# Turning twelve tiles on TensorE, a SyncE queue of transposes only, and a router per four tiles, in a fused layer of LayerNorm, attention and mixture of experts

## The chip, the cores and the metric

One Trainium2 chip, all 8 cores, every core with its own 4096 rows of the input and no traffic between cores. The time is the device time of the slowest core in microseconds (us). Lower is better. Weights and inputs are float32 in HBM; the matmuls run in bfloat16 with float32 sums.

## What is computed

The reference, cut to what matters (C = 1024, 16 heads of 64, 8 experts of width 128, shared expert of width 256, 6 of 8 experts taken):

```python
xn = (x - mean(x)) / sqrt(var(x) + 1e-5)
# attention on every 4th row of a segment of 2048 rows (512 rows), causal
q, k, v = split(xn[:, :, ::4] @ w_in.T + b_in)
a = softmax(causal(q @ k.T / 8)) @ v @ w_out.T + b_out      # other rows: 0
# feed-forward on every row
shared = (silu(xn @ ws1) * (xn @ ws2)) @ ws3
topk_w, topk_i = top_k(softmax(xn @ wr), 6);  topk_w /= sum(topk_w)
h = silu(xn @ w1[e]) * (xn @ w2[e])                         # all 8 experts
routed = sum_e w_full[:, e] * (h[e] @ w3[e])
out = x + a + shared + routed
```

## The kernel before

**Tiles.** The 4096 rows of a core are two segments of 2048; a tile is 128 rows, 32 tiles in all. `GROUPS` (line 30) puts four tiles of one residue together; tiles 12 to 15 and 28 to 31 are the rows on which attention runs, for segment 0 and 1.

**One order for all engines.** `steps()` (line 66) yields the steps of the whole program, and each engine's program is a loop over it that does its own part of each step. So every engine and every DMA queue works in the order of `steps()`, and a wait in one step holds back all that stands later on that engine.

**The steps.** `ln_stat` reads a tile of x (DVE statistics; ACT takes the square root with one table load, and the next silu needs another). `ln_norm` writes the normalised tile in bfloat16 to `xn_tm` (two buffers), and SP turns it by a DMA transpose into `XN` (line 321). `gu` is one unit of the first feed-forward matmuls: `s0` and `s1` are halves of the shared expert (264 and 256 columns, s0 with the 8 router columns), 0 to 3 are pairs of experts (512 columns). Each is 8 matmuls on PE (line 452) into one of six PSUM banks, a silu on ACT (line 690), a product on DVE (lines 602 and 629) into a piece buffer `hst`, and a DMA transpose by SP into `HT` (line 336): five transposes for each tile. The router (lines 585 to 620) runs on DVE once for each tile, in thirteen small operations. `down` multiplies `HT` by `W3` (line 472, 20 matmuls of 512 columns), and for attended tiles also `OFM` by `Wo` (line 476); DVE adds it to `res` (line 643). SP then stores `res` to out (line 356) and loads x into the `res` slot of tile m + 2 (line 311). `res` has three slots.

**Attention.** For each of 8 pairs of heads: `qk` (line 493), four `score` steps (lines 522, 525) with a maximum on DVE (line 660) and exp on ACT (line 724) into one of three `Pb` buffers, `pnorm` (DVE divides, line 670; SP turns the block by a DMA transpose into `PT`, line 349) and `av` of the pair before (line 543). One `down` step stands in each pair of heads, between `pnorm 2` and `pnorm 3`. So SP gets, in this order: transpose 2, the store and the load of `down`, transpose 3.

**Weights.** POOL starts all weight loads (they cast to bfloat16). `Wsh`, `Wgu` 0 to 3 and `W3` are started at the beginning, one behind the other. `Wqk` and `Wv` follow when tile 15 is normalised, `Wo` when the units of tiles 4 to 11 are through. A partition's row of a weight tensor is one contiguous run in HBM: 16 KB for `Wgu` and `Wv`, 8 KB for `Wqk`, 40 KB for `W3`. Loads of x are in runs of 4 KB.

**The order around the change.** LayerNorm of tiles 0 to 3; `s0`, `s1` of tiles 0 to 3 (with LayerNorm of 4 to 7); units 0 of tiles 0 to 7, units 1, then 2 and 3 for tiles 0 to 11, with the LayerNorm of later tiles in between; `down` 0 to 3; attention of segment 0 with `down` 4 to 11; tiles 12 to 27; attention of segment 1 with `down` 20 to 27; tiles 28 to 31 and their `down`.

## Times and profile before

| | us |
|---|---|
| median of 3 runs | 822.77 (821.97 to 835.91) |
| profiled execution, its own time | 831.12 |
| its span on the slowest core (core 3) | 829.6 |
| spans of the other cores | 801.2 to 819.5 |
| PE busy in that span | 614.3 (74%) |
| DVE busy | 377.4 (45%) |
| ACT busy | 248.7 (30%) |

The profile is of one execution, on its slowest core. PE is the matmul queue of TensorE, DVE is VectorE, ACT is ScalarE, POOL is GpSimd and SP is SyncE; SPq is SP's queue issuing DMAs. Times in rows count from the start of the span. The granted clock (PEclk) is 1.00 at 2.4 GHz and 0.5 at 1.2 GHz, averaged over a stretch. "Idle before, releaser" says what ended the idle time of an engine. The chain of waits is followed back from the last instruction to whatever released it.

### The profile page before, as it was taken

How to read it: one execution, taken by the hardware profiler on the slowest of the kernel's cores; microseconds unless marked ns; L12 is line 12 of the kernel's file. 1: busy time of each engine (PE TensorE's matmuls, PEld its weight loads, DVE VectorE, ACT ScalarE, POOL GpSimd, SP SyncE). 2: the span in 40 equal slices, each digit the busy share in tenths (PEclk: the TensorE clock that was granted, in tenths of full speed). 3: DMA queues.
4: the chain of work that ended last, by engine and by line, in shares of the span. 5: the costliest groups of instructions: out<-in, count | busy, mean ns of one | idle time of the engine just before them, and what ended most of it. 6: DMA issues, size and time to landing. Idle time of an engine off the chain costs nothing.

```text
span 829.6 us, 12117 instructions; the slowest of 8 cores (801.2 to 829.6 us)
## 1 busy us (share of the span) xinstructions
PE 614.3 (74%) x3136; PEld 294.6 (36%) x3136; DVE 377.4 (45%) x1232; ACT 248.7 (30%) x620; POOL 36.3 (4%) x48
## 2 busy tenths in 40 slices
PE   0006497898049689665699999998839878758998
PEld 0004153443014234322345445554414334323543
DVE  2006575754021444335354556766643545534531
ACT  0003425344001434233333224334423434332200
POOL 3000000001000000000101100000000000011002
PEclk9998899999569899879799999999979999877999
DMA  8996526349998977997326545664424975553123
GB/s 181 185 173 166 112 52 138 70 111 150 117 102 212 153 124 138 139 135 179 82 60 163 144 112 146 172 153 104 109 56 84 172 153 120 123 116 81 38 71 101
DMA packets 140866, 103.60 MB, mean 125 GB/s; under 512 B 124912, under 2 KB 124928, under 8 KB 139392
## 3 DMA queue, kind: packets, MB, share of 16 engines
q1 hardware_dynamic: 136704, 79.73, 44.6%
q0 software_dynamic: 4096, 23.10, 18.3%
q8 instruction: 28, 0.46, 0.3%
q14 instruction: 38, 0.31, 0.2%
HBM read 79.21 MB, written 16.78 MB: 116 GB/s over the span
## 4 chain that ended last, share of the span: by engine, by line
PE 43%; DMA 22%; DVE 11%; SPq 10%; issue 8%; ACT 5%; DVEq 1%; ACTq 0%
PE PS L452 17%; PE PS L472 14%; DMA PT<-Pb 14%; SPq L336 7%; DMA XF<-x 7%; PE PS L476 3%; ACT L690 3%; DVE bns L558 3%; PE PS L493 2%; PE PS L504 2%; DVE hst L629 2%; PE PS L543 2%; DVE res L643 1%; SPq L321 1%; PE PS L522 1%
## 5 line engine op out<-in xcount | busy, mean ns | idle before, releaser
L452 PE MATMUL PS<-Wgu,XN 128*128 128x512 bf16 x768 | 178.6, 392 | 12.1 <-DVE hst L602 7.5
L472 PE MATMUL PS<-W,HT 128*128 128x512 bf16 x560 | 135.9, 398 | 0.0
L629 DVE SCALAR_TENSOR_TENSOR hst<-sil,gate,PS 128x128 bf16<-128x128 bf16 x256 | 72.6, 343 | 100.5 <-ACT sil L690 56.7
L452 PEld LDWEIGHTS PS<-Wgu,XN 128*128 128x128 bf16 x768 | 76.5, 100 | 106.3 <-issue 26.1
L724 ACT ACTIVATE Pb<-PS,nmx 128x128 bf16<-128x128 f32 (+3 forms) x128 | 66.1, 524 | 134.9 <-DMA PT<-Pb 69.4
L452 PE MATMUL PS<-Wsh,XN 128*128 128x264 bf16 (+1 forms) x384 | 48.0, 281 | 67.6 <-DMA XN<-xn_tm 63.5
L660 DVE TENSOR_REDUCE nmx<-PS 128x2 f32<-128x256 f32 (+1 forms) x64 | 51.1, 819 | 80.1 <-PE PS L525 80.1
L690 ACT ACTIVATE sil<-PS 128x256 bf16<-128x256 f32 (+1 forms) x192 | 60.6, 349 | 80.3 <-PE PS L452 68.9
L472 PEld LDWEIGHTS PS<-W,HT 128*128 128x128 bf16 x560 | 57.0, 103 | 69.0 <-issue 11.9
L643 DVE TENSOR_TENSOR res<-PS,res 128x512 f32<-128x512 f32 x64 | 43.7, 690 | 82.4 <-PE PS L472 40.3
L493 PE MATMUL PS<-XN,Wqk 128*128 128x512 bf16 x256 | 65.3, 414 | 12.3 <-DMA XN<-xn_tm 12.3
L452 PE MATMUL PS<-Wgu,Wo 128*128 128x512 bf16 x256 | 60.6, 395 | 12.7 <-DVE hst L629 9.5
L681 ACT ACT_TABLE_LOAD x28 | 35.9, 1283 | 100.8 <-DVE rs L566 90.0
L452 PEld LDWEIGHTS PS<-Wsh,XN 128*128 128x128 bf16 x384 | 38.1, 100 | 78.9 <-issue 69.7
L543 PE MATMUL PS<-PT,Vs 128*64 128x256 bf16 x192 | 17.0, 332 | 49.2 <-DMA PT<-Pb 49.2
L690 ACT ACT_TABLE_LOAD x30 | 38.5, 1283 | 26.0 <-PE PS L452 25.6
L472 PE MATMUL PS<-W,PT 128*128 128x512 bf16 x80 | 19.7, 410 | 33.0 <-DMA PT<-hst 32.5
L493 PEld LDWEIGHTS PS<-XN,Wqk 128*128 128x128 bf16 x256 | 26.5, 106 | 45.0 <-issue 22.6
L452 PEld LDWEIGHTS PS<-Wgu,Wo 128*128 128x128 bf16 x256 | 25.5, 101 | 44.6 <-issue 18.0
L670 DVE TENSOR_SCALAR Pb<-Pb,rz 128x128 bf16<-128x128 bf16 (+3 forms) x128 | 33.9, 308 | 6.9
L706 ACT ACTIVATE Ks<-PS,bqk_sb 128x512 bf16<-128x512 f32 x16 | 11.0, 687 | 84.0 <-PE PS L493 83.9
L522 PE MATMUL PS<-Ks,Qs 64*128 64x128 bf16 (+3 forms) x128 | 22.1, 341 | 18.8 <-ACT Pb L724 18.8
(60 smaller groups left out, 466.8 us busy)
## 6 DMA issues: line engine op xcount, KB each, us to landing
res<-x SPq DMA_DIRECT2D x32, 512.0 KB, 5.8
out<-res SPq DMA_DIRECT2D x32, 512.0 KB, 3.6
XF<-x SPq DMA_DIRECT2D x24, 512.0 KB, 4.8
Wqk<-wqk POOLq DMA_DIRECT2D x16, 512.0 KB, 6.9
Wqk<-x SPq DMA_DIRECT2D x8, 512.0 KB, 5.3
Wgu<-wgu POOLq DMA_DIRECT2D x4, 1024.0 KB, 30.7
Wv<-wv POOLq DMA_DIRECT2D x4, 1024.0 KB, 14.6
W<-w POOLq DMA_DIRECT2D x1, 2560.0 KB, 54.4
```

Of the source, the lines that this page charges most:

```text
L336: sy.dma_start_transpose(out=ht_at(n)[:, b:b + 2, :], in_=hst[:, i % NPIECE, :]).then_inc(d_h[i % NPIECE], 16)
L452: ins = t_.matmul(PS[:, b, 0:nk], xn[:, ci, :], w[:, ci, k0:k0 + nk], start=(ci == 0), stop=(ci == CI - 1))
L472: ins = t_.matmul(PS[:, h, :], ht[:, k, :], W3[:, k, cols], start=(k == 0), stop=(k == NB - 1 and not 0 <= attended < 4))
L493: ins = t_.matmul(PS[:, b, :], Wqk[:, n % NWQK, ci, 128 * k:128 * (k + 1)], XN[:, s0:s0 + 4, ci, :], start=(ci == 0), stop=(ci == CI - 1))
L543: ins = t_.matmul(PS[64 * h:64 * (h + 1), b, 256 * half + q0:256 * (half + 1)], Vs[:, c, 128 * hp + 64 * h:128 * hp + 64 * (h + 1)], PT[:, ...
L629: ins = v.scalar_tensor_tensor(h[:, 128 * k:128 * (k + 1)], s[:, 128 * k:128 * (k + 1)], gate[:, n % 16, e:e + 1], PS[:, b, 256 + 128 * k: ...
L643: v.tensor_tensor(res[:, sl, cols], PS[:, h, :], res[:, sl, cols], op=ALU.add).then_inc(v_add, 1)
L660: v.tensor_reduce(nmx[:, i % 4, :], PS[:, b:b + 2, 0:128 * (j + 1)], axis=AX, op=ALU.max, negate=True).then_inc(v_mx, 1)
L670: ins = v.tensor_scalar(out=pp, in0=pp, scalar1=rz[:, i % 4, h:h + 1], scalar2=None, op0=ALU.mult)
L681: s.activation(out=sd[:, n % 4:n % 4 + 1], in_=mv[:, n % 4, 1:2], func=AF.Sqrt, bias=EPS).then_inc(a_sd, 1)
L690: s.activation(out=sil[:, i % 4, 0:nk], in_=PS[:, b, 0:nk], func=AF.Silu).then_inc(a_sil, 1)
L724: s.activation(out=Pb[:, i % NPB, 0:j + 1, h, :], in_=PS[:, b + h, 0:128 * (j + 1)].rearrange("p (c k) -> p c k", c=j + 1), func=AF.Exp, b ...
```

## The change

- **Turning.** The normalised tiles 0 to 15 are turned on PE (8 transposes of 128x128 for each tile, into bank 0 or 1) and evicted by ACT (new steps `xt`). For tiles 0 to 11 the pieces `s1`, 0 and 1 are turned on PE too (2 transposes each, step `ht`, evicted by ACT); pieces 2 and 3 of these tiles stay DMA transposes. For tiles 12 to 31 the four pieces of the experts go in one DMA transpose of 128x1024 and the shared piece in another: two for each tile in place of five.
- **Queues.** SP issues transposes only, but for the first four loads of x. All other loads of x, the loads of `res` and the stores of out are issued by POOL.
- **Router.** `s0` of four tiles, then one ranking for all four, then `s1` of four tiles with the gate behind the first: 12 operations of DVE and one tanh for four tiles, and four copies of the router columns.
- **LayerNorm.** From tile 4 on two tiles share one square root on ACT. Tiles 16 to 19 are normalised inside the attention of segment 0.
- **Attention.** `pnorm 3` stands ahead of `down`.
- **Weights.** Every weight is laid out in HBM so that a run is 4 KB. The loads are spread over the steps, `Wqk` has two buffers for three, `Wo` is loaded after the attention of segment 0.

```diff
+BATCH = [(0,), (1,), (2,), (3,)] + [(n, n + 1) for n in range(4, NTILE, 2)]
+def shared_steps(g):
+    for n in range(4 * g, 4 * g + 4):
+        yield ("gu", n, "s0")
+    yield ("rank", g)
+    for n in range(4 * g, 4 * g + 4):
+        yield ("gu", n, "s1")
+        if n == 4 * g:
+            yield ("gate", g)
...
         yield ("pnorm", seg, hp, 2)
+        yield ("pnorm", seg, hp, 3)
         yield ("down", fill + hp)
-        yield ("pnorm", seg, hp, 3)
+        if seg == 0 and hp in (1, 4):
+            yield ("ln_stat", BATCH_OF[16 + 2 * (hp == 4)])
+        if seg == 0 and hp in (2, 5):
+            yield ("ln_norm", BATCH_OF[16 + 2 * (hp == 5)])
...
+    yield ("w", "u1")
+    yield from shared_steps(0)
+    yield ("ht", 0, "s1")
     for n in range(4):
         yield ("gu", n, 0)
+        if n < 3:
+            yield ("ht", n + 1, "s1")
+        if n % 2 == 0:
+            yield ("ln_stat", BATCH_OF[4 + n])
+            yield ("ln_norm", BATCH_OF[4 + n])
+        else:
+            yield ("xt", 3 + n)
+            yield ("xt", 4 + n)
+        if n > 0:
+            yield ("ht", n - 1, 0)
...
+    for g in range(3, 7):
+        yield from shared_steps(g)
+        if g == 3:
+            yield ("av", 0, 7)
+        for n in range(4 * g, 4 * g + 4):
+            for u in range(4):
+                yield ("gu", n, u)
+                if g > 3 and n % 2 == 0 and u == 0:
+                    yield ("ln_stat", BATCH_OF[n + 4])
+                if g > 3 and n % 2 == 0 and u == 2:
+                    yield ("ln_norm", BATCH_OF[n + 4])
+            if g in (4, 5):
+                yield ("down", n - 4)
...
+def by_pe(n, u):
+    return n < 12 and u in ("s1", 0, 1)
...
 # SP
-                    elif st == "down":
-                        (m,) = at
-                        sy.wait_ge(v_add, 2 * m + 2)
-                        sy.dma_start(out=o_of(m), in_=res[:, m % NRES, :]).then_inc(d_out[m % NRES], 16)
-                        if m + 2 < NTILE:
-                            load_res(m + 2)
+                        elif u == 3:
+                            k = H_AT[(n, 0)][1]
+                            sy.wait_ge(v_h, GU_NO[(n, u)] + 1)
+                            sy.dma_start_transpose(
+                                out=ht_at(n)[:, 0:8, :],
+                                in_=hse[:, k:k + 4, :].rearrange("p a b -> p (a b)")).then_inc(d_h[("e", k)], 16)
...
 # POOL
-                    gp.dma_start(out=Wqk[:, n % NWQK], in_=dwqk[n % 8]).then_inc(d_wqk[n % NWQK], 16)
+                    gp.dma_start(out=Wqk[:, n % NWQK].rearrange("p (a b) k -> p a b k", a=2),
+                                 in_=dwqk[n % 8].rearrange("a p b k -> p a b k")).then_inc(d_wqk[n % NWQK], 16)
...
+                    if st == "ln_norm":
+                        for n in BATCH[at[0]]:
+                            k = n + 4 if n < 14 else n + 2
+                            if n in (14, 15) or k >= NTILE:
+                                continue
+                            gp.wait_ge(v_xn, n + 1)
+                            load_x(k)
...
                     elif st == "down":
+                        gp.wait_ge(v_add, 2 * m + 2)
+                        gp.dma_start(out=o_of(m), in_=res[:, m % NRES, :]).then_inc(d_out[m % NRES], 16)
+                        if m + 2 < NTILE:
+                            load_res(m + 2)
...
 # PE
+                    elif st == "xt":
+                        t_.wait_ge(v_xn, n + 1)
+                        bank_wait(b)
+                        for ci in range(CI):
+                            ins = t_.transpose(ps_bf16(b)[:, ci, :], xn_tm[:, n % 2, P * ci:P * (ci + 1)], ident[:])
+                        ins.then_inc(p_tr, 1)
+                    elif st == "ht":
+                        t_.wait_ge(v_h, GU_NO[(n, u)] + 1)
+                        bank_wait(b)
+                        for k in range(2):
+                            ins = t_.transpose(ps_bf16(b)[:, k, :], h_at(n, u)[:, P * k:P * (k + 1)], ident[:])
+                        ins.then_inc(p_tr, 1)
...
 # ACT
+                    elif st == "xt":
+                        s.wait_ge(p_tr, i + 1)
+                        s.activation(out=xn_at(n), in_=ps_bf16(i % 2), func=AF.Identity).then_inc(a_tr, 1)
```

In the stretch from unit 1 of tiles 0 to 7 on, the pairs of `ln_stat` and `ln_norm` stand behind the units of tiles 1 and 3 (unit 1) and 2 and 6 (unit 2), and their two `xt` steps one unit later (unit 1) or two units later (unit 2).

## Rows read from the trace of the kernel before

**Rows 1.** Busy time by stage; columns: stretch, each engine's busy us, clock, DMA share, GB/s
```profile
0.00:62.10 62.10, 0.00 (x0) 0.03 (x1) 7.91 (x18) 2.10 (x5) 6.38 (x19) 1.00 0.98 179
62.10:259.00 196.90, 136.66 (x656) 67.46 (x657) 93.66 (x349) 59.02 (x122) 2.65 (x5) 0.85 0.65 121
259.00:413.70 154.70, 114.03 (x602) 51.18 (x601) 65.16 (x170) 52.88 (x157) 9.96 (x12) 0.87 0.83 139
413.70:621.90 208.20, 187.15 (x969) 94.42 (x968) 121.47 (x444) 73.18 (x154) 4.69 (x2) 0.97 0.50 122
621.90:761.00 139.10, 111.75 (x601) 50.60 (x602) 65.93 (x168) 53.04 (x157) 7.89 (x8) 0.88 0.63 126
761.00:829.60 68.60, 64.67 (x312) 30.91 (x311) 23.24 (x85) 8.54 (x25) 4.70 (x2) 0.97 0.24 65
```

**Rows 2.** Timeline of the start; columns: start us, us, engine, line, instruction
```profile
18.00 1.28 DVE L558 BATCH_NORM_STATS2 bns<-Wqk 128x6 f32<-128x512 f32 x2 [7.00 <-DMA Wqk<-x]
...
21.76 36.88 SPq L321 DMA_TRANSPOSE XN<-xn_tm  x1
25.83 1.29 DVE L558 BATCH_NORM_STATS2 bns<-Wqk 128x6 f32<-128x512 f32 x2 [5.26 <-DMA Wqk<-x]
...
62.10 7.30 PE L452 MATMUL PS<-Wsh,XN 128*128 128x264 bf16 x48 [62.10 <-DMA XN<-xn_tm]
```

**Rows 3.** Timeline ahead of the first down step
```profile
239.09 15.21 PE L472 MATMUL PS<-W,PT 128*128 128x512 bf16 x60 [32.55 <-DMA PT<-hst]
```

**Rows 4.** Chain of waits in attention of segment 0; columns: start us, us, what
```profile
381.56 0.74 PE PS L543 x12
382.30 0.32 PE PS L522 x2
382.62 0.22 PE PS L525 x2
382.84 4.33 PE PS L472 x20
...
389.01 5.11 DMA PT<-Pb
```

**Rows 5.** Chain of waits: matmuls in a row at either level of the clock
```profile
259.19 3.45 PE PS L493 x16
...
287.85 5.14 PE PS L493 x16
```

**Rows 6.** Chain of waits in tiles 12 to 19
```profile
486.66 8.68 PE PS L452 x48
495.34 4.32 PE PS L472 x20
```

**Rows 7.** Timeline of DVE in tiles 24 to 27
```profile
559.68 1.28 DVE L558 BATCH_NORM_STATS2 bns<-XF 128x6 f32<-128x512 f32 x2
...
561.50 0.81 DVE L570 TENSOR_SCALAR xn_tm<-XF,mv,rs 128x1024 bf16<-128x1024 f32 x1 [0.18 <-DVE rs L566]
...
570.47 1.28 DVE L558 BATCH_NORM_STATS2 bns<-XF 128x6 f32<-128x512 f32 x2
```

**Rows 8.** Timeline of one unit behind PE, in units 3 of tiles 0 to 11
```profile
199.78 0.38 ACT L690 ACTIVATE sil<-PS 128x256 bf16<-128x256 f32 x1 [1.34 <-PE PS L452]
200.41 0.61 DVE L629 SCALAR_TENSOR_TENSOR hst<-sil,gate,PS 128x128 bf16<-128x128 bf16 x2 [1.12 <-ACT sil L690]
```

**Rows 9.** DMA issues of the page; columns: count, KB written each, median us to landing
```profile
res<-x SPq DMA_DIRECT2D x32, 512.0 KB, 5.8
out<-res SPq DMA_DIRECT2D x32, 512.0 KB, 3.6
...
Wgu<-wgu POOLq DMA_DIRECT2D x4, 1024.0 KB, 30.7
...
W<-w POOLq DMA_DIRECT2D x1, 2560.0 KB, 54.4
```

**Rows 10.** Busy time of core 5 in the dense stretch; columns as in Rows 1
```profile
454.00:540.00 86.00, 86.00 (x455) 44.35 (x454) 52.41 (x188) 31.85 (x67) 0.00 (x0) 1.00 0.60 157
```

More of the change, by code:

```diff
@@ L89, in steps @@
+    yield ("ht", 7, 1)
+    yield ("w", "u3")
+    yield ("w", "w3")
+    yield from shared_steps(2)
+    yield ("ht", 8, "s1")
+    for u in (0, 1):
+        for n in range(8, 12):
+            yield ("gu", n, u)
+            if u == 0 and n < 11:
+                yield ("ht", n + 1, "s1")
+            if n > 8:
+                yield ("ht", n - 1, u)
+            elif u == 1:
+                yield ("ht", 11, 0)
     for n in range(12):
         yield ("gu", n, 2)
-        if n % 3 == 2:
-            yield from ln_step(12 + n // 3)
+        if n == 0:
+            yield ("ht", 11, 1)
+        if n in (2, 6):
+            yield ("ln_stat", BATCH_OF[12 + (n == 6) * 2])
+            yield ("ln_norm", BATCH_OF[12 + (n == 6) * 2])
+        if n in (4, 8):
+            yield ("xt", 12 + (n == 8) * 2)
+            yield ("xt", 13 + (n == 8) * 2)
@@ L284, in build_nc @@
         a_av = sem("a_av")
+        a_tr = sem("a_tr")
         def wait_x(eng, n):
[L287 to L299 removed]
+            if n < 4:
+                eng.wait_ge(d_x0[n], 16)
+            elif n < 16:
+                eng.wait_ge(d_x[n % 4], 16 * (n // 4))
+            else:
+                eng.wait_ge(d_x[n % 2], 16 * (3 + (n - 16) // 2 + 1))
         with nc.Block() as block:
@@ L622, in _ @@
[L622 to L626 removed]
+                        else:
+                            v.wait_ge(v_zg, 7 * (n // 4) + 7)
                             for k in range(2):
```

463 lines of the change are left out of this document (267 added, 196 removed).

## The prediction, made before the changed kernel was run

> **What bounds the kernel now.** I read the busy time by stage first, since one share for the whole span says nothing of where PE waits [rows 1]. PE is idle for 62 us, then busy 136.7 of 196.9 us at a granted clock of 0.85. It is nearly full only in tiles 12 to 27 and at the end. Both attention stages leave 27 to 41 us idle, at a clock below 0.9. So the question in each stage is what PE waits for.
>
> The timeline of the start shows it [rows 2]. Tiles 0 and 1 are normalised early, but SP sits for 36.88 us on one transpose, and the first matmul begins at 62.10. Meanwhile POOL's queue moves Wsh, four Wgu and W3; W3 lands 54.4 us after its issue [rows 9]. Tiles 2 and 3 of x are there only at 18.00 and 25.83. The same happens ahead of the first `down`: PE waits 32.55 us for a transpose of a piece [rows 3], just when Wqk, Wv and Wo are being loaded.
>
> In attention the chain of waits goes in a ring: `down` on PE 4.33, the addition on DVE, then SP's store and load, then the transpose 5.11, then `av`, a score, `down` again [rows 4]. The transpose of score 3 is held by `down`, which it doesn't need. In tiles 12 to 19 the chain is PE alone: 8.68 us for a tile's six units and 4.32 for `down` [rows 6]. In tiles 24 to 27 a tile takes 10.79 us (570.47 less 559.68), since router and LayerNorm stand on DVE between two tiles [rows 7].
>
> **The floor of PE at full clock.** A tile's units 8.68; `down` 4.32 for 20 matmuls, for an attended tile 16 more, so 7.78 [rows 6]; `qk` 3.45 and a `v` half of it, 1.73 [rows 5]; a 128-column matmul 0.11, 0.22 for two [rows 4].
> Tiles 0 to 11: 12 x 8.68 = 104, `down` 4 x 4.32 = 17. Added: `xt` of tiles 4 to 15, 12 x 8 x 0.11 = 11, and 36 `ht` steps of two, 36 x 2 x 0.11 = 8. Together 140.
> One attention stage: 8 x 3.45 + 8 x 1.73 + 8 x 4.32 = 76, scores and `av` some 19 (32 scores with masks, on average 0.4 from the longest at 0.54; 8 `av` at 0.74) [rows 4]: 95.
> Tiles 12 to 27: 16 x 8.68 + 4 x 7.78 + 4 x 4.32 = 187. End: 65 busy [rows 1].
> Sum 140 + 95 + 187 + 95 + 65 = 582.
>
> **The start: 62 becomes 20.** x in runs of 4 KB lies beside weights in runs of 16 KB. Tiles 2 and 3 (1.05 MB) came in from about 8 to 25.8 us, 59 GB/s, while all loads to 62 us (weights 15.8 MB, bias and six tiles 3.6 MB) went at about 312 GB/s [rows 2, 9]. That is a fifth of the whole, as if the queues took turns run by run. With runs of 4 KB on both sides x gets half: 1.05 MB at 156 GB/s is 7 us, tile 3 is there at 15.5; Wsh (2.1 MB) at about 16. Statistics, root, normalising (1.3 + 0.2, 0.5, 0.8) and the turn of tile 3 with its eviction take 4.5: first unit at 20. All four `xt` stand before the first unit, so the last tile counts. If the runs change nothing, tile 3 comes at 25.8 and the first unit at 30.6; if only the last tile of x counts, 18. I take 20.
>
> **Stage to the first `qk`: 197 becomes 180.** PE needs 140. Against it stands a new wait. An `xt` needs the tile normalised, and PE works in order. A unit's product is done about 1.45 us after PE has left it (silu 0.38, products 0.61, gaps) [rows 8]. Then DVE does two tiles' statistics (2 x 1.28 + 0.4), waits for the root behind a table load (1.6), and normalises (0.2 + 0.81) [rows 7]: 5.7, so 7.2 us after the unit. PE has one unit and one or two `ht` (1.95 to 2.2) until the first `xt` in four cases, two units (3.5) in two. Waits 4 x 5.2 + 2 x 3.7 = 28. Each also costs clock: after a wait 16 matmuls took 5.14 against 3.45 [rows 5], 1.7; for six about 9. Eviction of a whole turned tile isn't in the trace: between one silu of 256 columns, 0.38, and four of them, 1.5 [rows 8]; 16 of these are 6 to 24 us on ACT, which is busy 59 of 197 [rows 1] and loses table loads. I take 1.1, off the path; uncovered, it adds 1.1 at the start and nothing behind. The 24 transposes left to SP for pieces 2 and 3 run beside W3. Eight piece buffers give them eight units (13.8 us) of slack; beyond that a late transpose holds DVE. The 32.55 goes: `down` 0 to 3 need pieces sent 20 us or more earlier. `down` 2 and 3 still wait some 3 us for `res`, whose load follows the store. 140 + 28 + 9 + 3 = 180. Bounds: 143 with the waits filled, 195 if DVE is two units behind each time.
>
> **Attention of segment 0: 155 becomes 115.** `pnorm 3` no longer waits for `down` on DVE nor on SP. The ring is then `av` 0.8, score 0.5, maximum and exp about 3.0, division 0.9, transpose 5.1 to 5.9: 10.8 per pair of heads, against 95 / 8 = 11.9 of PE. PE bounds, narrowly. I add 1.3 for each pair (10), 4 for two LayerNorm batches with two changes of table each (4 x 1.28, half of it beside other work), 4 for Wv and Wqk at the beginning and 2 for the clock. Bounds: 103 and the 155 of before.
>
> **Tiles 12 to 27: 208 becomes 190.** 187, and 3 for the change from attention. The router falls from 13 operations a tile to 16 for four tiles and the root to one table pair for two, so 10.79 goes to 8.68. Its latency lies under four `s1` units and the six banks. Behind the rank DVE still has 52 of 86 us [rows 10]. **Attention of segment 1: 139 becomes 111**, as before but with no LayerNorm. **End: 69 stays**; PE is the chain there, and the last store through POOL may cost half a microsecond.
>
> **Sum.** 20 + 180 + 115 + 190 + 111 + 69 = 685 of span, against 829.6. The profiled execution took 831.12, the median of the runs is 822.77: 1% lower. So 685 x 822.77 / 829.6 = 679.
>
> **Edits at nothing.** Stores and loads through POOL: POOL is busy 36 of 830 us and what it then waits for (an addition, a product of `qk`) comes in the same order as on PE. What stands behind a waiting `down` on POOL is the next Wqk load and the next x; two buffers of Wqk and two to four of x leave them a pair of heads, 12 us. If that cover were gone, each late Wqk load costs its whole landing.
>
> **Rivals.** (a) *Attention stays at its pace.* The ring was never held by order but by the DMA engines: their share is 0.83 and 0.63 there [rows 1], and the same bytes in less time raise it. For it: it would be 0.83 x 155 / 115, above 1, in segment 0. Against: that share held Wo (4 MB), now elsewhere, and time in which runs wait for each other; in the dense stretch 0.60 was enough for 153 GB/s [rows 10]. It gives 155 + 139 in place of 115 + 111: 679 + 67 = 746.
> (b) *The clock gives way* when all cores are full at once. At the 0.85 seen in [rows 1] the 582 us of PE become 685: 782. Against it: in the dense stretch core 5 ran 86.00 of 86.00 us at 1.00 [rows 10], all others like it.
> The Trainium skill, "TensorE: Matmul & The Clock Gate", Part 1, says that three or more cores of a die with dense matmuls take the die to thirteen sixteenths of the clock. By that rule the sum would be 134 us more, 813, not faster by 2%. The trace does not agree: 1.00 over 86 us.
> (c) *Slower: the `res` ring through POOL.* A slot of `res` is stored, then loaded, in one queue with all weights; three tiles take one store and one load. Now 3.6 + 5.8 [rows 9], no bound. If each of POOL's transfers takes L, a tile takes 2L/3. The first `down` comes at about 180; the kernel is slower once 32 tiles need more than 650 us, 20.3 each, L = 30.6. That is the landing of a Wgu at the start, 30.7 [rows 9]: then 180 + 32 x 20.5 = 836 of span, 829. Against it: such times belong to a queue filled with 15 MB.
> The Trainium skill, "SBUF — State Buffer", section "SBUF: two separate sides", says that descriptors of POOL's transfers are held up while DVE works in a mode with both ports. It gives no price for this mix; it speaks for (c), and no row here shows such a hold.
> (d) *The runs of 4 KB don't help*, and transposes beside weights stay slow: start 30.6, 10 more in both stages before tile 12: 710.
>
> **Chances.** Forecast 0.62, own range 645 to 712, from its bounds: waits in stage two filled (-30) or longer (+15), attention +-8 each. (d) 0.11. (a) 0.16, (b) 0.06, (c) 0.03, and 0.02 for a small change through something not seen. Two per cent is about what a measurement of this kernel can tell from no change. (a), (d) and, but for 0.01 of it with a still lower clock, (b) are faster by more: 0.62 + 0.11 + 0.16 + 0.05 = 0.94. Within 2% 0.03 (that 0.01 and the unseen 0.02), slower 0.03. Range 642 to 746: up to (a), leaving out (b), (c) and half of (a).
>
> **What would show it.** First unit near 20 us (start right); waits of PE for DVE's normalising, six of 3.5 to 5.5 us; no long wait ahead of `down` 0; `down` steps 12 to 13.5 us apart in attention, with the chain on PE; tile periods of 8.7 in tiles 24 to 27. Wrong if PE waits for `PT` in most pairs of heads (a), if the granted clock is under 0.95 where PE is full (b), if DVE waits for `res` or for x from POOL (c), or if x lands after 25 us (d).

## The result, and the profile after

The changed kernel is faster, by much less than forecast. Its median is 763.45 us of 4 runs (760.16 to 766.15) against 827.33 us of 4 runs of the kernel before beside them (821.97 to 835.91): a ratio of 0.925, 95% interval 0.916 to 0.934. The prediction was 679 us, range 642 to 746. The direction was right; the size was not.

Busy time by stage of the changed kernel on its slowest core (core 7, span 758.6), cut at the same marks as [rows 1]; columns as there:
```profile
0.00:21.10 21.10, 3.75 (x32) 3.07 (x33) 9.47 (x20) 4.78 (x8) 6.79 (x19) 1.00 0.89 176
21.10:205.00 183.90, 148.90 (x828) 80.52 (x827) 74.79 (x229) 66.06 (x144) 15.16 (x26) 0.90 0.62 121
205.00:366.60 161.60, 117.11 (x642) 54.23 (x640) 75.05 (x195) 59.34 (x168) 22.75 (x34) 0.83 0.84 151
366.60:569.50 202.90, 184.71 (x928) 91.78 (x928) 88.10 (x270) 47.23 (x110) 20.86 (x29) 0.96 0.69 118
569.50:691.30 121.80, 108.68 (x641) 51.51 (x642) 65.58 (x176) 53.76 (x162) 16.03 (x24) 0.96 0.81 150
691.30:758.60 67.30, 60.50 (x273) 26.90 (x272) 15.23 (x40) 6.83 (x17) 10.24 (x9) 0.96 0.23 66
```

The marks behind each attention need care: up to `av` of the last pair the kernel before had one unit to do, the changed one has eight (some 7 us of PE), so these rows carry them in the attention. At marks that mean the same in both (the first unit behind the last `qk`), on the same two cores:

| stage | before, core 3 | after, core 7 | change | predicted change | miss |
|---|---|---|---|---|---|
| start | 62.1 | 21.2 | -41 | -42 | +1 |
| to the first `qk` | 196.9 | 183.7 | -13 | -17 | +4 |
| attention of segment 0 | 143.7 | 151.7 | +8 | -40 | **+48** |
| tiles 12 to 27 | 219.3 | 212.9 | -6 | -18 | +12 |
| attention of segment 1 | 130.4 | 111.8 | -19 | -28 | +9 |
| end | 77.3 | 77.3 | 0 | 0 | 0 |
| span | 829.6 | 758.6 | -71 | -145 | +74 |

The start gave what was promised, and the stage behind it nearly. Core 3 was the longest of the kernel before in the second and the third stage, so this pair of cores flatters both: by the medians over all cores (next section) the changes are -43, -9, +16, -6, -20 and +1. Attention of segment 0 gave nothing: it is the stage in which LayerNorm, all four kinds of loads and the transposes of P lie together, at a DMA share of 0.84 and the lowest clock, 0.83. Its chain of waits (columns as in [rows 4]), where the transposes of P stand:
```profile
219.44 8.00 DMA PT<-Pb
...
268.59 10.17 DMA PT<-Pb
...
294.36 23.30 DMA PT<-Pb
317.67 0.35 issue
318.01 1.28 PE PS L704 x12
...
332.55 10.23 DMA PT<-Pb
```
The transpose of [rows 4] took 5.11 us; here the chain meets 8 to 23 us, and DMA of P is 32.0% of this stage's chain, 52 us. The waits of the same stretch say the same from the side of ACT and PE (columns: engine, line, waited for: us in total, times, longest us):
```profile
ACT Pb L906 <- DMA PT<-Pb: 37.0, 6, 7.8
...
PE PS L683 <- ACT Pb L906: 24.7, 6, 6.8
...
PE PS L704 <- DMA PT<-Pb: 15.3, 1, 15.3
```
The typical transpose of P is hardly slower than before: over all cores the median in this stage, from issue to landing, was 5.5 us and is 5.7. The late ones became more: 39 of 249 took over 10 us against 14 of 248, and 21 took over 12 us against 6.

In some executions one die showed a lower granted clock than the other and took longer: the ratios below leave these out, the medians do not, and where the profiled one was such (b1, e10, g2, f1, a0) its stages were read on the other die too, and the text gives attention 0 there where it differs by over 2 us.

### The profile page after: what moved, and what is told of

Same layout as the page of the kernel before. It is cut to its first block, busy times and chain, and to the rows that moved or that the text cites. A ratio compares the mean times of both kernels' runs of the same rounds, so it can differ in the third digit from the quotient of the medians.

```text
span 758.6 us, 11591 instructions; the slowest of 8 cores (735.3 to 758.6 us)
## 1 busy us (share of the span) xinstructions
PE 623.7 (82%) x3336; PEld 308.0 (41%) x3336; DVE 328.2 (43%) x930; ACT 238.0 (31%) x608; POOL 91.8 (12%) x140
## 4 chain that ended last, share of the span: by engine, by line
PE 50%; DMA 20%; DVE 12%; issue 8%; ACT 6%; SPq 2%; DVEq 1%; ACTq 0%; POOLq 0%; POOL 0%
PE PS L589 25%; DMA PT<-Pb 11%; PE PS L633 10%; PE PS L656 4%; PE PS L637 4%; DMA HT<-hse 3%; PE PS L667 3%; ACT Pb L906 3%; DVE bns L720 3%; DMA XN<-xn_tm 3%; DMA Wqk<-x 2%; PE PS L602 2%; SPq L426 2%; DVE xn_tm L737 1%; PE PS L704 1%
## 5 line engine op out<-in xcount | busy, mean ns | idle before, releaser
L589 PE MATMUL PS<-Wgu,XN 128*128 128x512 bf16 x768 | 174.3, 386 | 4.4 <-DVE hse L798 4.4
L798 DVE SCALAR_TENSOR_TENSOR hse<-sil,gate,PS 128x128 bf16<-128x128 bf16 x256 | 76.1, 343 | 159.8 <-ACT sil L860 141.8
L633 PE MATMUL PS<-W,HT 128*128 128x512 bf16 x560 | 131.1, 388 | 1.5 <-DVE res L812 1.5
L860 ACT ACTIVATE sil<-PS 128x256 bf16<-128x256 f32 (+1 forms) x192 | 64.0, 349 | 203.8 <-PE PS L589 177.6
L633 PEld LDWEIGHTS PS<-W,HT 128*128 128x128 bf16 x560 | 55.4, 100 | 67.3 <-issue 7.5
L589 PE MATMUL PS<-Wsh,XN 128*128 128x256 bf16 (+1 forms) x384 | 47.0, 286 | 8.7 <-DMA XN<-xn_tm 8.7
L555 POOL DMA_DIRECT2D out<-res x32 | 17.9, 561 | 287.2 <-DVE res L812 286.8
L602 PE MATMUL PS<-ident,xn_tm 128*128 128x128 bf16 x128 | 15.2, 308 | 45.3 <-DVE xn_tm L737 45.3
L683 PE MATMUL PS<-Ks,Qs 64*128 64x128 bf16 (+3 forms) x128 | 21.2, 326 | 34.6 <-ACT Pb L906 34.5
L835 DVE RECIPROCAL rz<-zz 128x2 f32<-128x2 f32 x64 | 10.4, 162 | 76.4 <-ACT Pb L906 76.4
L507 POOL DMA_DIRECT2D XF<-x x22 | 11.7, 532 | 207.6 <-DVE xn_tm L737 206.5
```

The source lines that it names most:

```text
L589: ins = t_.matmul(PS[:, b, 0:nk], xn[:, ci, :], w[:, ci, k0:k0 + nk], start=(ci == 0), stop=(ci == CI - 1))
L602: ins = t_.transpose(ps_bf16(b)[:, ci, :], xn_tm[:, n % 2, P * ci:P * (ci + 1)], ident[:])
L633: ins = t_.matmul(PS[:, h, :], ht[:, k, :], W3[:, k, cols], start=(k == 0), stop=(k == NB - 1 and not 0 <= attended < 4))
L798: ins = v.scalar_tensor_tensor(h[:, 128 * k:128 * (k + 1)], s[:, 128 * k:128 * (k + 1)], gate[:, n % 16, e:e + 1], PS[:, b, 256 + 128 * k: ...
L860: s.activation(out=sil[:, i % 4, 0:nk], in_=PS[:, b, 0:nk], func=AF.Silu).then_inc(a_sil, 1)
```

## How the runs are compared

All stage times below are medians over the eight cores of one profiled execution, in us, at marks that can be found alike in every kernel: the first unit, the first `qk`, the first unit behind the last `qk`, the first `qk` of segment 1, the first unit behind its last `qk`, the end. The cores of one run lie within 4 us of each other at the start, but within 4 to 24 us in attention 0 (widest in e7, 140.8 to 164.3). So I read differences of 7 and more between medians, and take smaller ones as a hint only; attention 0 of b1 (111.6 to 133.4) and of b2 (135.9 to 153.1) do not overlap. Kernels of one batch ran on one chip, and each ratio is to the runs of before in its own batch, whose median was 835.6 to 841.4; so medians of different batches are not compared, ratios are. The 161 and 122 us in the expectations of e1 to e4 are the attention stages of core 7 up to `av` of the last pair, as in the rows above; in the table they are 148.6 and 112.0.

| kernel | start | to `qk` | att. 0 | 12-27 | att. 1 | end | median | ratio to before |
|---|---|---|---|---|---|---|---|---|
| before | 63.4 | 187.6 | 132.3 | 218.5 | 131.7 | 76.6 | 827.33 | 1 |
| after | 20.4 | 179.0 | 148.6 | 213.0 | 112.0 | 77.2 | 763.45 | 0.925 |
| a0 after again | 20.8 | 182.7 | 149.7 | 211.8 | 113.0 | 77.4 | 768.03 | 0.912 (.902-.923) |
| b1 before + new order | 63.6 | 189.0 | 124.8 | 212.9 | 112.9 | 71.8 | 792.97 | 0.944 (.931-.958) |
| b2 = b1 + POOL's queue | 65.6 | 183.5 | 142.9 | 214.7 | 115.9 | 79.8 | 817.70 | 0.980 (.969-.990) |
| b3 before + short runs | 30.2 | 204.3 | 133.6 | 217.7 | 131.4 | 77.5 | 801.29 | 0.962 (.952-.972) |
| e2 after, long runs | 31.1 | 183.3 | 159.2 | 213.2 | 115.8 | 81.8 | 797.28 | not given |
| e10 after, old order | 20.5 | 188.5 | 153.8 | 213.4 | 140.9 | 75.6 | 813.89 | not given |
| e1 after, x/res/out on SP | 21.0 | 184.8 | 137.9 | 208.5 | 111.3 | 75.9 | 753.57 | 0.900 (.887-.912) |
| e3 after, LayerNorm out | 20.4 | 181.1 | 129.7 | 223.3 | 118.6 | 77.5 | 760.84 | 0.906 (.889-.923) |
| e9 after, no table change | 20.5 | 187.3 | 146.0 | 210.8 | 111.8 | 77.3 | 776.17 | 0.927 (.914-.941) |
| e4 after, no `Wqk` reloads | 20.6 | 179.3 | 130.1 | 211.8 | 107.2 | 80.0 | 748.01 | 0.889 (.875-.903) |
| e6 after, bare attention | 20.7 | 180.1 | 103.9 | 224.2 | 104.9 | 80.1 | 725.04 | 0.861 (.851-.871) |
| e7 after, four `Pb` | 20.7 | 180.5 | 147.5 | 210.4 | 109.4 | 77.3 | 772.86 | 0.913 (.901-.925) |
| e5 after, five transposes | 20.7 | 178.9 | 152.1 | 200.5 | 117.7 | 77.3 | 757.24 | 0.903 (.897-.910) |
| f1 = e1 + e5 | 21.0 | 185.1 | 140.8 | 207.2 | 107.8 | 76.1 | 753.84 | 0.900 (.887-.912) |
| f2 = f1, loads deferred | 21.0 | 184.0 | 134.5 | 207.3 | 110.4 | 76.8 | 746.90 | 0.889 (.878-.901) |
| g1 = f2, LayerNorm moved | 21.3 | 202.4 | 110.0 | 207.4 | 109.7 | 76.6 | 744.93 | 0.890 (.875-.905) |
| g2 = g1, moved further | 21.1 | 196.4 | 111.9 | 207.8 | 110.8 | 76.0 | 737.43 | not given |
| g3 = g2, `res` 2 early | 20.9 | 194.0 | 108.6 | 207.8 | 110.4 | 76.2 | 731.68 | 0.883 (.873-.894) |

a0 shows how well a kernel repeats itself: up to 4 us in a stage, and 0.912 against 0.925 in the ratio.

## Experiments on the steps that held

**b1: the new order alone**, in the kernel before.
```diff
         yield ("pnorm", seg, hp, 2)
-        yield ("down", fill + hp)
         yield ("pnorm", seg, hp, 3)
+        yield ("down", fill + hp)
```


> The kernel before with one part of the change alone: pnorm 3 ahead of down in each pair of heads. The prediction took the ring (down, addition, SP's store and load, transpose 3, av) as what bounds attention, with 5.7 us of it removable by this order. Theory O (order): both attention stages shorter by 25 us or more together, ratio 0.97 or less. Theory B (the transposes come late because other transfers run beside them): under 10 us together, ratio 0.985 to 1.0.

Attention 0 went from 132.3 to 124.8, attention 1 from 131.7 to 112.9, the ratio to 0.944. One moved line is worth more than half of the whole change's gain. So the order did hold the attention of segment 1. In attention 0 its 7.5 us are no more than the cores differ among themselves, and 124.8 is still some 20 above the forecast, whose 115 is 104 at these marks (11 us less, as 154.7 and 143.7 on core 3). That stage had something else in it even with the old queues and no LayerNorm inside.

**e10: the changed kernel with the old order.** The same two lines put back.

> The changed kernel with the down-projection ahead of the fourth normalising, as before. b1 showed the swap to give 7.5 us in attention 0 and 18.8 us in attention 1 in the kernel before. If it is worth as much here, attention 0 is 156 to 160 and attention 1 126 to 134, 25 to 35 us in all, ratio .955 to .965. If in attention 0 the late transfers bound the pace whatever the order (theory: TensorE waits for the turned P there, not for its bank), attention 0 stays at 149 to 153 and only attention 1 grows by 12 to 19; ratio .94 to .95.

Attention 1 grew by 28.9, attention 0 by 5.2 (2.1 on cores 4 to 7), and the best run was 799.89. Core 5, whose mean granted clock of 0.915 is among those of the changed kernel's cores (0.914 to 0.935), has 141.4 in attention 1, so the growth is not the clock's. In the changed kernel the order is worth even more in attention 1, and nothing that can be told from noise in attention 0: there something else was the bound.

**b3: short runs alone**, in the kernel before: all weight arrays in runs of 4 KB, e.g.
```diff
-                    gp.dma_start(out=Wgu[:, u], in_=dwgu[u]).then_inc(d_wgu[u], 16)
+                    gp.dma_start(out=Wgu[:, u].rearrange("p (a b) k -> p a b k", a=4),
+                                 in_=dwgu[u].rearrange("a p b k -> p a b k")).then_inc(d_wgu[u], 16)
```


> The kernel before with the weight arrays laid out in 4 KB runs and nothing else. If runs of 4 KB give the activations beside them a larger share (forecast, and e2's +11 us at the start when undone), the fourth tile of x lands 5 to 10 us earlier, the time to the first unit falls from 63 to 50 to 57, and attention 0 is 5 to 10 us shorter than 132; ratio .965 to .985. If the share doesn't hang on the run length, the ratio is 1.00 +- .01.

The first unit came at 30.2 in place of 63.4, far more than I expected. The timeline of SP's queue shows why (columns as in [rows 2]); the transpose whose issue took 36.88 us there takes 11.08:
```profile
16.15 11.08 SPq L321 DMA_TRANSPOSE XN<-xn_tm  x1
27.28 2.84 SPq L323 DMA_DIRECT2D XF<-x  x1
30.83 17.09 SPq L321 DMA_TRANSPOSE XN<-xn_tm  x1
```
But the next ones still take 17.09, and the stage to the first `qk` gives 17 of the 33 back. Attention did not move (133.6), against my 5 to 10.

**e2: the changed kernel with the old long runs.** b3's edit the other way round.

> The changed kernel with the weights laid out in HBM as before (runs of 8 to 40 KB in place of 4 KB). If short runs are what lets transposes and loads of x through: first unit at 28 to 31 us in place of 21, attention of segment 0 longer by 10 or more, kernel 780 to 800. If short runs cost DMA time (more packets for the same bytes) and that is the loss in attention: attention of segment 0 shorter by 10 or more, kernel under 755.

Start 31.1 against 20.4, attention 0 +10.6 (+4.6 on cores 4 to 7), in all 27 us of span. The statistics of the fourth tile of x begin at 26.33 with long runs and at 16.43 with short ones (first row e2's, second row the changed kernel's timeline):
```profile
26.33 1.29 DVE L716 BATCH_NORM_STATS2 bns<-Wqk 128x6 f32<-128x512 f32 x2 [4.26 <-DMA Wqk<-x]
```
```profile
16.43 1.29 DVE L720 BATCH_NORM_STATS2 bns<-Wqk 128x6 f32<-128x512 f32 x2 [0.55 <-DMA Wqk<-x]
```
With b3 this is a small square: the kernel before 63, short runs alone 30, all of the change but short runs 31 (turning on TensorE, and the weight loads spread over the steps, which no run parts), all of it 20. Either side removes most of the long wait; together they add only 10 more.

## Experiments on the step that failed

Three suspects for attention 0: the transfers of x, `res` and out now in POOL's queue; the weight reloads beside them; LayerNorm of tiles 16 to 19 inside.

**e6: attention without the last two.** No reloads of `Wqk` and `Wv` (all heads use the weights that were loaded first), LayerNorm with its loads of x moved behind the attention. The loads of `res` and the stores of out stay in POOL's queue.
```diff
-                        if n + NWQK < 16:
-                            load_wqk(n + NWQK)
-                        if kc == 3 and i < 3:
-                            load_wv(i + 1)
-        if seg == 0 and hp in (1, 4):
-            yield ("ln_stat", BATCH_OF[16 + 2 * (hp == 4)])
-        if seg == 0 and hp in (2, 5):
-            yield ("ln_norm", BATCH_OF[16 + 2 * (hp == 5)])
```


> The changed kernel with most of what runs beside the transposes of P taken out of attention: only two of 16 loads of Wqk and one of four of Wv are made (later heads use those weights, so this part of the result is not the reference's), and the LayerNorm of tiles 16 to 19 stands in the units of tiles 12 to 15. Singly, no Wqk took 18.5 us off the attention of segment 0 and no LayerNorm 19. Theory B+L (competing transfers and LayerNorm together are the whole loss): 149 falls by 38 or more, to 105 to 112, what the forecast had (115 less the last av). Theory R (the ring of three P buffers with a latency of 5 us for each transpose bounds by itself): it stays at 118 or more, and segment 1 at 105 or more.

Attention 0 fell from 148.6 to 103.9. The run's slowest core in that stretch (columns as in [rows 1]) and its waits for P:
```profile
205.00:309.00 104.00, 97.78 (x559) 44.28 (x567) 59.49 (x148) 49.78 (x151) 10.79 (x17) 0.97 0.62 132
```
```profile
ACT Pb L896 <- DMA PT<-Pb: 9.8, 6, 2.9
```
TensorE is busy for 98 of 104 us, and no transpose of P took over 8 us on any core. So the work of attention itself has the pace I forecast, and the miss is what lies beside it. Eight loads of `res` and eight stores went through POOL's queue here too: by themselves they cost nothing that shows. The next ones part it.

**b2: POOL's queue alone**, on top of b1.
```diff
 # SP
-                        sy.dma_start(out=o_of(m), in_=res[:, m % NRES, :]).then_inc(d_out[m % NRES], 16)
-                        if m + 2 < NTILE:
-                            load_res(m + 2)
 # POOL
+                        gp.wait_ge(v_add, 2 * m + 2)
+                        gp.dma_start(out=o_of(m), in_=res[:, m % NRES, :]).then_inc(d_out[m % NRES], 16)
+                        if m + 2 < NTILE:
+                            load_res(m + 2)
```
The loads of x from tile 4 on move in the same way.

> The kernel before with the fourth normalising ahead of the down-projection (as in b1) and, new, all loads of x from tile 4 on, of the residual and all stores issued by GpSimd; the weight loads keep their long runs. If the move to GpSimd's queue costs by itself (theory), attention of segment 0 is 5 to 15 us longer than b1's 124.8, the transpose of a normalised tile takes 6 us or more instead of 3.1, and the ratio is .955 to .98 against b1's .944. If the move is free, as the forecast had it, attention 0 is 125 +- 3 and the ratio .944 +- .01. The first tiles may start later too, since x of tiles 4 to 7 now stands behind the weights in GpSimd's order; that is read from the first stages and kept apart.

Attention 0 went from 124.8 to 142.9, the ratio from 0.944 to 0.980. No byte more is moved, no wait is added on SP, and in neither run does PE wait for a load of `Wqk` in that stage, on any core. The DMA issues of the two pages, first b1, then b2 (columns: what, queue, count, KB written each, median us to landing):
```profile
res<-x SPq DMA_DIRECT2D x32, 512.0 KB, 5.9
...
Wqk<-wqk POOLq DMA_DIRECT2D x16, 512.0 KB, 7.6
...
HT<-hst SPq DMA_TRANSPOSE x140, 2.4
...
PT<-Pb SPq DMA_TRANSPOSE x64, 4.6
...
XN<-xn_tm SPq DMA_TRANSPOSE x24, 3.1
```
```profile
res<-x POOLq DMA_DIRECT2D x32, 512.0 KB, 6.8
...
Wqk<-wqk POOLq DMA_DIRECT2D x16, 512.0 KB, 10.2
...
HT<-hst SPq DMA_TRANSPOSE x140, 2.4
...
PT<-Pb SPq DMA_TRANSPOSE x64, 5.9
...
XN<-xn_tm SPq DMA_TRANSPOSE x24, 5.9
```
The transpose of a normalised tile lands in 5.9 us in place of 3.1; in attention 0 alone that of P goes from 5.0 to 7.3. The transposes of the pieces (`HT`), on whose signal no plain transfer starts, keep their 2.4 us, though most of them lie outside the attention: not every transpose is slower for sharing the DMA engines with POOL's queue. This is an edit that the prediction put at nothing.

The Trainium skill, "DMA: Bandwidth & Descriptors", section "Issuing engines are not separate DMA queues", says that transfers issued from different engines interleave on the same DMA engines and that using several issuers only saves issue time. These two runs show more: who issues decides what a transfer lies beside (3.1 against 5.9 us, and 18 us in the stage). Its section "Queues, rings and completion order" says that a DMA engine takes turns between the queues that have work, a packet at a time. By that rule a transpose shares its turns with whatever POOL's queue holds at that moment. The rows of `XN` and P agree, but would also agree with plain collisions in time (below).

**e1: the changed kernel with these transfers back on SP.** The reverse of b2's edit, and the loads of x behind SP's transposes.

> The changed kernel with one part undone: the loads of x and res and the stores of out are issued by SP again, in the order of the steps. In the changed kernel the attention of segment 0 takes 161 us where 115 were forecast. Theory Q (two queues take turns on the DMA engines, so a transpose that used to be alone behind plain transfers of its own queue now shares every turn with them): attention of segment 0 falls to 140 or less, the median transpose of P lands in under 5 us, the kernel takes 740 or less. Theory B (the DMA engines are simply full of bytes in that stage): 161 stays within 5, kernel 763 +- 8. Theory S (SP's order was the loss in the kernel before): SP waits for additions again, attention of segment 1 goes from 122 back towards 139, kernel 780 or more.

Attention 0 148.6 to 137.9, tiles 12 to 27 213.0 to 208.5, ratio 0.900; the 740 us that the expectation gave for this theory did not come (753.57). The transpose of a normalised tile (first e1's row, then the changed kernel's):
```profile
XN<-xn_tm SPq DMA_TRANSPOSE x16, 3.3
```
```profile
XN<-xn_tm SPq DMA_TRANSPOSE x16, 8.6
```
On SP a load of x is issued behind the transpose; on POOL it starts on the same signal, `v_xn`, beside it. Whether the queue or the simultaneous start costs the 5 us is not settled: both change together in b2 and in e1.

**e3: LayerNorm out of attention**, to the units of tiles 12 to 15.
```diff
-                if g > 3 and n % 2 == 0 and u == 0:
+                if n % 2 == 0 and u == 0:
                     yield ("ln_stat", BATCH_OF[n + 4])
```


> The changed kernel with the LayerNorm of tiles 16 to 19 (four loads of x, two changes of the ACT table there and back, four transposes) taken out of the attention of segment 0 and put into the units of tiles 12 to 15. Theory L (this work is what holds attention): attention of segment 0 falls from 161 to 135 or less, kernel 745 or less. Theory B (bytes): 3.1 of 24.4 MB go, 161 falls by 10 to 20 and tiles 12 to 27 give part of it back, kernel 750 to 760. If neither: 161 +- 5.

Attention 0 148.6 to 129.7, but tiles 12 to 27 213.0 to 223.3 and attention 1 +6.6. LayerNorm costs the attention 19 us, not the 4 of the sum, and the two stages behind give 17 of them back (760.84, ratio 0.906; the time of theory B and not of theory L). It does not act by making P land later. In attention 0 alone, on the slowest core, first e3, then the changed kernel:
```profile
PT<-Pb SPq DMA_TRANSPOSE x31, 5.4
```
```profile
PT<-Pb SPq DMA_TRANSPOSE x31, 5.5
```
and ACT's waits for P there, as the median over the cores, are 41 us in e3 and 37 in the changed kernel.

**e9: the same LayerNorm without its change of table.** The root of tiles 16 to 19 is replaced by a copy on ACT, so that no table is loaded.
```diff
+                        fn = AF.Identity if BATCH[k][0] in (16, 18) else AF.Sqrt
```


> The changed kernel in which the root of tiles 16 to 19 is replaced by a plain copy, so that ACT changes no table in the attention of segment 0; these four tiles are then scaled wrongly, and nothing else changes (same loads, same transposes, same DVE work). Taking the whole LayerNorm out had shortened that stage by 19 us. Theory T (the two changes of table in the row of exps): at least 8 of the 19 come back here. Theory B (its 3 MB of loads and transposes): under 4.

146.0 against 148.6 (148.2 and 142.2 on the two dies): the table is little or nothing of the 19. What remains is DVE's own work in order ahead of the division of P, four more transposes ahead of P's in SP's queue, and four loads of x; which of the three weighs most wasn't tried singly. In the changed kernel's chain of waits both of the first two stand right ahead of a late transpose of P:
```profile
263.46 0.82 DVE xn_tm L737
264.41 1.62 SPq L426
...
266.18 2.26 SPq L426
...
268.59 10.17 DMA PT<-Pb
```

**e4: no reloads of `Wqk`.**
```diff
-                        if n + NWQK < 16:
-                            load_wqk(n + NWQK)
```


> The changed kernel in which only the first two of the 16 loads of Wqk are made; the later pairs of heads use the weights of the first two, so 14 MB of reads are left out and all engines' work stays. Theory B (bytes): attention of segment 0 falls from 161 by 25 to 45, of segment 1 from 122 to about 105, kernel about 700 to 720. Theory L (LayerNorm's changes of table and DVE time in attention): 161 falls by less than 10. Theory Q: falls by 10 to 20, since one of two competing streams is halved.

All later pairs of heads use the first two `Wqk`. 130.1: 18.5 us less, with LayerNorm and POOL's queue as they were. Here P does land sooner: ACT's waits for it halve, from 37 to 19 us (medians over the cores), and 17 transposes in place of 72 take over 8 us. Attention 1 gains 4.8. LayerNorm and these reloads are 37.5 of the 44.7 us that e6 takes out; the two reloads of `Wv` and the interplay hold the other 7. The 11 us of e1 do not belong to that sum, since e6 leaves `res` and out in POOL's queue: what that queue costs hangs on what else is there.

**e7: four `Pb` buffers.** `NPB = 3` becomes 4, in case ACT only lacked a place to write.

> The changed kernel with four P buffers in place of three, nothing else. Theory R (ACT waits for the buffer of three scores before, so every late transpose stops the scores): attention of segment 0 falls by 10 or more, of segment 1 by 4 or more, kernel 745 to 753. Theory B (the DMA engines can't deliver sooner): both within 4, since PE then waits for the same transposes in av.

147.5: nothing. Though ACT is recorded as waiting for the transpose to free `Pb`, a fourth buffer doesn't help, since `av` needs the same transposes a moment later: ACT's waits for P fell from 37 to 28 us and PE's rose from 13 to 20 (medians over the cores). The wait row named the right transfer and the wrong remedy.

**e5: the four pieces of tiles 12 to 31 turned one by one again.**
```diff
-                            sy.dma_start_transpose(
-                                out=ht_at(n)[:, 0:8, :],
-                                in_=hse[:, k:k + 4, :].rearrange("p a b -> p (a b)")).then_inc(d_h[("e", k)], 16)
+                            sy.dma_start_transpose(out=ht_at(n)[:, 2 * u:2 * u + 2, :], in_=h_at(n, u)).then_inc(
+                                d_h[H_AT[(n, u)]], 16)
```


> The changed kernel with one part undone: from tile 12 on the four expert pieces of a tile go in four DMA transposes of 128x256 again, in place of one of 128x1024. In the changed kernel tiles 12 to 27 take 13 us more than forecast, with DVE waiting 8.7 us for such a large transpose and PE 8.7 us for a tile behind it in SP's queue. Theory M (merging makes bursts that come late and hold the two-tile ring of pieces): that stage falls by 5 to 13 us. Theory B (the same bytes beside the same POOL loads): within 3. SP's issues alone, 4 x 1.25 in place of 1.3 a tile, are no bound in either.

Tiles 12 to 27: 200.5 against 211.8 in a0, its neighbour; attention 0 and 1 are 2 and 5 us longer, and the ratio, 0.903 against 0.912, moves by less than its interval. The changed kernel's chain has, in tiles 20 to 27,
```profile
481.62 17.35 DMA HT<-hse
...
509.68 15.99 DMA XN<-xn_tm
...
547.67 7.33 DMA HT<-hse
```
and e5's has of these only those of `XN` (14.46 us the longest). The merged transpose can start only behind the fourth product and frees four of the eight places at once, and DVE waited for it, 17.9 us in three waits in that stage:
```profile
DVE hse L798 <- DMA HT<-hse: 17.9, 3, 8.7
```

## Putting the causes right

**f1** is e1 and e5 together, but POOL's weight loads still wait for the normalising, as in the changed kernel (in e1 that wait had gone with the loads of x); **f2** loads `Wqk` and `Wv` of segment 1 in tiles 24 to 27 instead of at the end of attention 0.

> The two undone parts that each helped, together: loads of x and res and stores on SP (12 us off the median span of a core), with POOL still held by v_xn so that the weights are spread as in the changed kernel, and five transposes for each tile from 12 on (11 us off tiles 12 to 27). If they add up: median span of a core 728 to 735 against 752, kernel 735 to 745 with a before of 827, ratio 0.88 to 0.89. If both act through the same waits: ratio 0.895 or more.

> f1_combo with the loads for segment 1 that stand in the attention of segment 0 (Wv for its first half, two Wqk, 4 MB read) moved to the units of tiles 24 to 27. Leaving out 7 Wqk loads of that stage gave 18.5 us, 2.6 us for each MB. Theory B: attention of segment 0 shorter by 8 to 12 than in f1, tiles 12 to 27 longer by at most 3, ratio lower by 0.007 to 0.012. Theory L (only what is loaded next to LayerNorm matters): under 3.

f1 gave no more than e1 (0.900; its attention 0 is 137.0 on cores 0 to 3): e5's gain in tiles 12 to 27 is smaller once x is on SP's queue behind the transposes (207.2, e1 alone 208.5). f2 brought attention 0 to 134.5, 6 us less (2 on cores 0 to 3) where 8 to 12 were expected, and the ratio to 0.889. In that stage P lands in 3.8 us where the changed kernel has 5.5 (first f2, then the changed kernel, issues of attention 0 alone):
```profile
PT<-Pb SPq DMA_TRANSPOSE x31, 3.8
```
```profile
PT<-Pb SPq DMA_TRANSPOSE x31, 5.5
```
and still the stage is 31 us above the 103.9 of e6. LayerNorm is what is left in it, with six of the eight reloads of `Wqk` and one of `Wv`.

**g1: LayerNorm of tiles 16 to 19 among the units of expert pair 3**, ahead of the attention, on top of f2.
```diff
     for n in range(12):
         yield ("gu", n, 3)
+        if n in (4, 8):
+            yield ("ln_stat", BATCH_OF[16 + 2 * (n == 8)])
+        if n in (6, 10):
+            yield ("ln_norm", BATCH_OF[16 + 2 * (n == 10)])
```


> All work done, three causes mended together: activations' transfers issued by SyncE again, pieces of the gated product turned one by one, the weights of segment 1 loaded in tiles 24 to 27, and LayerNorm of tiles 16 to 19 put into the twelve units of expert pair 3 instead of into the attention. If the loss in attention 0 was the sum of these (theory), it falls from f2's 134.5 to 112 to 122, tiles 12 to 27 stay at 207 +- 5, and the ratio is .865 to .88. If LayerNorm's cost only moves with it, the stage before attention grows by 8 or more and the ratio is .885 to .90 as in f2.

Attention 0 at 110.0: with no load or step left out, it is within 6 us of the forecast (104 at these marks), though six reloads of `Wqk` and one of `Wv` are still in it. The 18.5 us of e4 were a price beside LayerNorm and POOL's transfers. But the stage before it grew by 18.4, and the total stands still (0.890). The chain there shows what for: behind SP's transposes a load of x, then LayerNorm, then store and load of `res`:
```profile
192.50 0.51 SPq L417
193.11 5.58 DMA XF<-x
...
212.27 6.16 DMA out<-res
218.49 7.57 DMA res<-x
```
**g2** takes the first pair's statistics to unit 1 and its normalising to unit 2, so that the load has time; **g3** also loads the third `res` tile with the first two.

> g1 with the statistics and the normalising of tiles 16 and 17 taken three and four units earlier (behind units 1 and 2 of expert pair 3 instead of 4 and 6), 18 and 19 unchanged, so that the load of x for tile 18, which may only start when tile 16 is normalised, has some 12 us before VectorE asks for it instead of 4. If the 18 us of g1 are the wait for that load and what stands behind it, the stage before attention falls from 202 to 188 to 194 and the ratio to .87 to .88. If it is the work of LayerNorm itself, it stays at 200 to 204 and the ratio at .89.

> g2 with the third residual tile loaded with the first two, ahead of the units of expert pair 3, instead of behind the store of the first down-projection. In g1 the chain before attention holds 6.2 us of a store and 7.6 us of a residual load. If these are on the path, the stage before attention is 5 to 8 us shorter than in g2; if another residual load only takes their place, within 2 us of it.

The stage went 202.4, 196.4, 194.0 (g2's attention 0 is 108.6 on cores 0 to 3): 6 us were the place of that load, 2.4 the `res` tile, about the "within 2" of a load that only takes another's place. Ten remain against f2: that is what two batches of LayerNorm cost here, less than half of the 24.5 us that the attention lost with them (f2 to g1). g3 is the fastest, 731.68 us, 0.883 (0.873 to 0.894), against 0.912 (0.902 to 0.923) and 0.925 (0.916 to 0.934) of the changed kernel's two batches. Its attention 0 on its slowest core, busy time and waits:
```profile
217.80:326.10 108.30, 99.87 (x565) 44.41 (x564) 60.41 (x151) 50.32 (x152) 7.19 (x8) 0.95 0.94 172
```
```profile
ACT Pb L912 <- DMA PT<-Pb: 11.5, 5, 5.0
```
The DMA share is higher than in the changed kernel (0.94 against 0.84), with 18.6 MB moved in place of 23.4 (medians over the cores), and the stage is 43 us shorter than 151.7 at the same marks: 37.0 us of ACT's waits for P became 11.5.

## Why the prediction was right or wrong

**Start: right.** Tile 3 of x was forecast at 15.5 and its statistics began at 16.43; first unit forecast 20, measured 21.19. With long runs in their place the text gave 25.8 and 30.6; e2 has 26.33 and 31.1. Eviction of a whole turned tile, bounded by 0.38 and 1.5 and taken as 1.1, took
```profile
13.54 1.02 ACT L871 ACTIVATE XN<-PS 128x1024 bf16<-128x1024 bf16 x1 [2.24 <-PE PS L602]
```

**To the first `qk`: right in its length, and for the stated reason.** The forecast was 180, measured are 183.7 on core 7 and 179.0 as the median; the gain by medians is 9 us and not 17, since core 3 of the kernel before was 9 above its median. Six waits of PE for the normalising, 4 x 5.2 + 2 x 3.7 = 28, were forecast:
```profile
PE PS L602 <- DVE xn_tm L737: 28.0, 6, 5.3
PE PS L633 <- DVE res L812: 3.7, 1, 3.7
```
Both the 28 and the 3 for `res` are there. The 32.55 ahead of the first `down` [rows 3] is gone.

**Attention of segment 0: wrong, and this is the miss.** The step that failed is the ring of 10.8 us against 11.9 of PE: its term "transpose 5.1 to 5.9" put one typical duration on the link whose late cases set the pace. With it failed "edits at nothing" for POOL's queue, the 4 us for LayerNorm with its changes of table, and the reloads of `Wqk`, which had no term at all (the 4 for `Wv` and `Wqk` was for the first loads). The typical duration was right, 5.7 over all cores. But 72 of 249 transposes took over 8 us, and those on the chain 8 to 23. That could be seen before: there 42 of 248 took over 8, the longest 24.3. The margin was 1.1 us for each pair, and I priced the link by a row of before, in a stage whose neighbours I was changing. b1 shows that the order alone, with the old neighbours, falls short too (124.8, not 104). b2 prices the move to POOL's queue at 18 us in the kernel before, e1 at 11 in the changed one. e3 prices LayerNorm at 19, and not through later landing of P; e4 the reloads of `Wqk` at 18.5. These prices hang on each other and are not to be added. I had looked at POOL as an engine (busy 36 of 830 us, what stands behind a waiting step) and not at what its transfers lie beside. The floor under it was right: without reloads and LayerNorm the stage took 103.9 (e6), and with no work left out 108.6 (g3). Those 45 us are most of the 48 of the table. Whether a transpose suffers from the second queue or from the transfer that starts with it stays open.

**Tiles 12 to 27: 12 too high a gain, attention 1: 9.** In the first, the merged transpose has no term in the sum; e5 gives it 11 us. In the second, the new order gives all that was gained (112.9 in b1, 112.0 in the changed kernel), and the reloads of the weights hold it back: 107.2 without those of `Wqk` (e4), 104.9 without any (e6). That is 7 of the 9. A slip in the range: its -30 for filled waits should have been -37 by its own bound of 143; nothing hangs on it.

**The rivals.** (a) named the right stage and the right suspects, the DMA engines, and its 155 for attention 0, no gain, is about what came. The amount moved does not explain it alone: b1 and b2 move 20.2 and 20.6 MB there in 124.8 and 142.9 us, the changed kernel and e1 both 23.4 MB in 148.6 and 137.9, and e4 and g3 19.3 and 18.6 MB in 130.1 and 108.6 (medians over the cores). What a transpose stands beside counts as well. (a) also foresaw no gain in attention 1, which gained 19. Its sign, PE waiting for `PT` in most pairs, was looked for on the wrong engine: PE waited for it once, ACT six times. (b) did not come: behind tile 16 core 0 ran at full clock, as all eight cores did in this stretch,
```profile
420.00:470.00 50.00, 50.00 (x265) 25.76 (x263) 24.57 (x74) 12.73 (x29) 9.54 (x14) 1.00 0.67 125
```
and the 0.83 of attention 0 stands where PE was busy for 117 of 161.6 us. (c) `res` lands in 6.8 us, not 30.6; but a price for POOL's queue between nothing and these 30.6 was never asked for. (d) fell by e2 and b3.

## What to carry to other kernels

When a ring of waits is only a tenth shorter than the engine that would take over, price its slowest link by its late cases and beside its new neighbours, not by one old row, and let the range reach to the case that it doubles. Moving transfers to another engine's queue is not free because that engine is idle: look at which small, urgent transfers (here transposes) will now start together with large ones. A price found by taking one neighbour away holds beside the others only: the reloads cost 18.5 us in the changed kernel and little in g3. And try the one-line change of order first: it gave more than half of the gain of the whole rewrite.

## What was not expected of the hardware

- Changing only which queue issues the plain transfers lengthened the landing of DMA transposes from 3.1 to 5.9 us (b1 to b2), and from 3.3 to 8.6 us (e1 to after); that of the smaller pieces stayed at 2.4 us (b1 to b2).
- The issue of one DMA transpose holds its queue: 36.88 us beside weight loads in long runs [rows 2], 11.08 in runs of 4 KB (b3), with the same bytes. The next one still took 17.09.
- A stage can have a DMA share of 0.94 and be faster than at 0.84 (g3 and the changed kernel, 18.6 and 23.4 MB), with TensorE busy for 100 of 108 us.
- The median of 249 transposes of P moved by 0.2 us between the two kernels (5.5 to 5.7) while those over 12 us went from 6 to 21.
